# A cross-attention and recurrence kernel: the recurrence's unit changes from four value columns of one chunk to two value columns of two chunks

## The reference, cut to what matters

```
def step(s, rkvw):
    r_t, k_t, v_t, w_t = rkvw
    a = k_t[:, :, :, None] * v_t[:, :, None, :]
    out = jnp.einsum('bhk,bhkd->bhd', r_t, u * a + s)
    return (a + w_t[:, :, :, None] * s, out)
_, outs = jax.lax.scan(step, s0, xs)
```

## Time and profile before

| | before |
|---|---|
| median of 3 runs (lowest, highest) | 2302.81 us (2302.04, 2303.87) |
| the profiled execution | 2301.0 us |
| its span, first to last instruction | 2299.2 us |
| mean granted TensorE clock | 0.967 |
| PE busy | 2141.9 us (93%), 14176 records |
| DVE busy | 1952.8 us (85%) |
| ACT busy | 1260.4 us (55%) |
| POOL busy | 585.2 us (25%) |
| DMA, mean | 30 GB/s |

### The profile page before, as it was taken

The page is one execution under the profiler, slowest core; times in us unless marked ns, Lnnn a source line. Parts: engine busy times, 40 slices in busy tenths (PEclk is TensorE's granted clock), DMA queues, the critical chain, the costliest instruction groups (busy, mean ns, idle before and its releaser), DMA issues. The chain is left out here.

```text
span 2299.2 us, 41734 instructions
## 1 busy us (share of the span) xinstructions
PE 2141.9 (93%) x14176; PEld 1477.2 (64%) x14176; DVE 1952.8 (85%) x4863; ACT 1260.4 (55%) x4405; POOL 585.2 (25%) x700
## 2 busy tenths in 40 slices
PE   3698799999999999999999999999999999999866
PEld 2475576767666676767667676766767676666533
DVE  0258898989899898989989898999989899998982
ACT  1736374573838466383746648373755738374312
POOL 1131314222331422232141322224141222314200
PEclk7799899999999999999999999999999999999977
DMA  7100101001010100001010100101010010100000
GB/s 268 35 7 20 31 11 49 11 11 41 11 50 11 49 11 31 21 11 50 11 49 11 48 3 11 50 11 50 11 49 1 11 50 11 50 2 29 1 19 10
DMA packets 48978, 69.88 MB, mean 30 GB/s; under 512 B 20512, under 2 KB 26656, under 8 KB 48768
## 3 DMA queue, kind: packets, MB, share of 16 engines
q1 hardware_dynamic: 48768, 67.21, 8.9%
HBM read 50.42 MB, written 16.78 MB: 29 GB/s over the span
## 5 line engine op out<-in xcount | busy, mean ns | idle before, releaser
L1226 DVE TENSOR_TENSOR_SCAN st<-ws,st 128x256 f32<-128x256 f32 x1024 | 637.4, 686 | 0.1
L862 ACT ACTIVATE probs_or_mixes<-probs_or_mixes,least 128x128 f32<-128x128 f32 x1024 | 398.9, 403 | 117.4 <-DVE least L1173 116.3
L1215 DVE TENSOR_TENSOR st<-bank_pair,kT 128x1016 f32<-128x1016 f32 x256 | 308.0, 1203 | 88.0 <-PE bank_pair L717 88.0
L1236 DVE TENSOR_TENSOR st<-st,rT 128x1024 f32<-128x1024 f32 x256 | 317.9, 1243 | 0.0
L1173 DVE CUSTOM_DVE_ANT_0 probs_or_mixes<-bank,nmask 128x128 f32<-128x128 f32 x1024 | 231.1, 285 | 100.5 <-PE bank L566 76.0
L1108 POOL TENSOR_SCALAR rstd<-rstd 128x1 f32<-128x1 f32 x96 | 26.5, 276 | 1098.4 <-ACT cin L895 600.1
L1102 POOL TENSOR_TENSOR probs_or_mixes<-probs_or_mixes 128x512 f32<-128x512 f32 x160 | 190.1, 1218 | 341.4 <-DVE probs_or_mixes L1267 341.4
L862 ACT ACTIVATION_READ_ACCUMULATOR probs_or_mixes<-probs_or_mixes,least 128x1 f32 x1024 | 206.4, 202 | 0.0
L717 PE MATMUL bank_pair<-v_hi,sel 32*128 32x256 f32 x1024 | 193.8, 339 | 10.9 <-DVE st L1215 10.6
L717 PE MATMUL bank_pair<-v_lo,sel 32*128 32x256 f32 x1024 | 166.6, 286 | 0.0
L717 PEld LDWEIGHTS bank_pair<-v_hi,sel 32*128 32x128 f32 x1024 | 114.5, 185 | 72.3 <-issue 35.4
(11 more groups left out here) (150 smaller groups left out, 4216.3 us busy)
## 6 DMA issues: line engine op xcount, KB each, us to landing
inputs_turned<-in_ctx_turned SPq DMA_DIRECT2D x16, 512.0 KB, 3.6
inputs_turned<-in_x_turned SPq DMA_DIRECT2D x16, 512.0 KB, 4.6
xin<-in_x SPq DMA_DIRECT2D x16, 512.0 KB, 3.7
x<-xin SPq DMA_DIRECT2D x16, 512.0 KB, 4.1
keep<-x SPq DMA_DIRECT2D x16, 512.0 KB, 3.6
out<-keep SPq DMA_DIRECT2D x32, 256.0 KB, 2.0
wo<-in_wo SPq DMA_DIRECT2D x2, 1024.0 KB, 11.3
nmask<-in_mask SPq DMA_DIRECT2D x16, 128.0 KB, 4.1
```

The source lines that it names most:

```text
L862: last = fn(pr[:, n % 4, j, :], pr[:, n % 4, j, :], ACT.Exp, bias=least[:, n, j:j + 1], scale=-1.0, accum_out=rsum[:, n, j:j + 1])
L1215: tt(dst, src, over(kv, DU, 1), ALU.mult).then_inc(outer.sem, 1)
L1226: last = nc.vector.tensor_tensor_scan(v, ws[:, c].rearrange("p b t -> p (b t)"), v, 0.0, ALU.mult, ALU.add)
L1236: tt(v, v, over(rT[:, u // PER, :], DU, 1), ALU.mult).then_inc(weighed.sem, 1)
```

## The change

**The unit.** A unit is now two value columns (`UNIT_D`) of two chunks (a half of the group's four chunks, called p). It still has 4 x 256 columns in a slot and there are still 16 units in a group, but a slot is now two rows of 512 columns, and a matmul or a scan covers both chunks of one value column at once. The spread is four matmuls of 512 columns instead of eight of 256, the scan two of 512 instead of four of 256, and the reduce four matmuls of 512 instead of eight of 256, into the whole of bank 7, over four reduces instead of two. The bonus moves to the ring of banks as a job of its own, twice a group with two matmuls, and the readout is done twice a group, at 512 columns, instead of four times. POOL's `rk` and `dg` are done in two pieces of 512 instead of four of 256, as two separate steps (`rk`, `joined`).

**Waits.** The first reduce of a half waits until the last readout has read bank 7 (`read_out`). The centred value weights at the start use banks 7 and 3 in turn instead of 7 and `pair`, so that the third matmul group waits for the first copy, the fourth for the second, and PE waits for all four copies before it goes on to `low` (before, it waited for them only at the first `proj_v`).

**Order.** All four lists are new. They are turned round (the period is cut at another place, so that some steps lost one of their lateness), and steps have moved against each other.

```diff
-UNIT_D = [(0, 1, 8, 9), (4, 5, 12, 13), (2, 3, 10, 11), (6, 7, 14, 15)]
+HALF_T = 2 * T
+UNIT_D = [(4 * (w % 2) + w // 2, 8 + 4 * (w % 2) + w // 2) for w in range(2 * PER)]
...
-reduce.4+2 spread.12+2 low_rank.0+1 spread.13+2 key.0 reduce.5+2 tdecay.0+1 spread.14+2 low_rank.2+1 proj_r.0+1
+low_rank.0+1 key.0 spread.13+2 tdecay.0+1 reduce.5+2 low_rank.2+1 spread.14+2 proj_r.0+1 decay.0+1 spread.15+2
...
-            if n % 2 == 0:
-                jobs.append((("readout", n // 2), READOUT, late))
+            keys = [("bonus", n // PER)] if n % PER == PER - 1 else []
...
-        spare = [bank[7][:], pair[:, 0], pair[:, 1], bank[7][:]]
+        spare = [bank[7][:], bank[3][:], bank[7][:], bank[3][:]]
...
-                    if e == 3:
-                        pe.wait_ge(centred_v, 1)
+                    if e >= 2:
+                        pe.wait_ge(centred_v, e - 1)
...
+                pe.wait_ge(centred_v, NC)
...
-                for k in range(2):
-                    for part in (v_hi, v_lo):
-                        for s in range(2):
-                            d = UNIT_D[u % PER][2 * s + k]
-                            r = slice(32 * (d // 4), 32 * (d // 4) + 32)
-                            last = mm(pair[:, s, k * T:(k + 1) * T], sel[r, d % 4, :], part[r, c, :],
-                                      start=part is v_hi, stop=part is v_lo)
+                p, w = u // (2 * PER), u % (2 * PER)
+                for part in (v_hi, v_lo):
+                    for half in range(2):
+                        d = UNIT_D[w][half]
+                        r = slice(32 * (d // 4), 32 * (d // 4) + 32)
+                        last = mm(pair[:, half, :], sel[r, d % 4, :],
+                                  part[r, 2 * p:2 * p + 2, :].rearrange("p c n -> p (c n)"),
+                                  start=part is v_hi, stop=part is v_lo)
...
-                m, c = q % 2, q // 2
+                p, m = q // PER, q % PER
                 if m == 0:
-                    bonus(g, c)
+                    wait(pe, read_out.sem, read_out.after(g, p))
+                if m == PER - 1:
+                    bonus(g, p)
                 pe.wait_ge(weighed.sem, weighed.after(g, 2 * q + 2))
...
+                for half in range(2):
                     for u in (2 * q, 2 * q + 1):
...
+                        r = 64 * half + 32 * (u % 2)
+                        last = mm(bank[7][r:r + 32, :], ebase[:, o:o + 32],
+                                  st[:, u % SLOTS, half * HALF_T:(half + 1) * HALF_T], start=m == 0, stop=m == PER - 1)
...
-                for s in range(DU):
-                    v = st[:, u % SLOTS, s * T:(s + 1) * T]
-                    last = nc.vector.tensor_tensor_scan(v, ws[:, c].rearrange("p b t -> p (b t)"), v, 0.0,
+                for half in range(2):
+                    v = st[:, u % SLOTS, half * HALF_T:(half + 1) * HALF_T]
+                    last = nc.vector.tensor_tensor_scan(v, ws[:, 2 * p:2 * p + 2].rearrange("p c b t -> p (c b t)"), v, 0.0,
...
-                tt(dg[:, c % 2, :], ps[:, T:2 * T], dg[:, c % 2, :], ALU.mult).then_inc(diag.sem, 1)
-                dve.wait_ge(diag.sem, diag.after(g, c + 1))
-                tt(att[:, c, :], ps[:, 0:T], dg[:, c % 2, :], ALU.add).then_inc(free, 1)
+                tt(dg[:], ps[:].rearrange("p (c n) -> p c n", c=2), dg[:], ALU.mult).then_inc(free, 1)
+                dve.wait_ge(summed.sem, summed.after(g, PER * (p + 1)))
+                dve.wait_ge(free, XB.through(("bonus", p), g))
+                tt(att[:, both, :], bank[7][:].rearrange("p (c n) -> p c n", c=2), dg[:], ALU.add).then_inc(read_out.sem, 1)
```

More of the change, by code:

```diff
@@ L127 @@
-values.1 turn_p.8 score.12 turn_p.9 turn_p.10 reduce.2+1 turn_p.11 score.14 spread.8+1 project.0 turn_m.1+2 values.2
-turn_p.12 turn_p.13 spread.9+1 turn_p.14 reduce.3+1 flip.1 turn_p.15 spread.10+1 share.1 values.3 project.1 ffn_k.0+2
-ffn_r.0+2 ffn_k.1+2 spread.11+1 ffn_r.1+2 turn_n.0 turn_n.1 ffn_v.0+2 ffn_v.1+2 low.0
+low_rank.0+1 key.0 spread.13+2 tdecay.0+1 reduce.5+2 low_rank.2+1 spread.14+2 proj_r.0+1 decay.0+1 spread.15+2
+proj_v.0+1 proj_k.0+1 reduce.6+2 decay.1+1 spread.0+1 reduce.7+2 query.0 var.0+2 proj_r.1+1 value.0 score.0
@@ new lines @@
+spread.1+1 rstd.0+2 proj_g.0+1 spread.2+1 score.2 proj_g.1+1 spread.3+1 query.1 turn_p.0 turn_p.1 reduce.0+1 score.4
+spread.4+1 turn_p.2 out.0+2 turn_p.3 spread.5+1 score.6 turn_p.4 out.1+2 values.0 reduce.1+1 score.8 spread.6+1
+turn_p.5 turn_p.6 proj_v.1+1 proj_k.1+1 turn_p.7 turn_m.0+2 spread.7+1 score.10 flip.0 reduce.2+1 values.1 turn_p.8
+score.12 turn_p.9 spread.8+1 share.0 turn_p.10 score.14 turn_p.11 spread.9+1 turn_m.1+2 project.0 reduce.3+1 values.2
+turn_p.12 turn_p.13 turn_p.14 flip.1 turn_p.15 share.1 values.3 spread.10+1 project.1 ffn_k.0+2 ffn_k.1+2 spread.11+1
@@ L130 @@
+ffn_r.0+2 ffn_r.1+2 turn_n.0 turn_n.1 ffn_v.0+2 ffn_v.1+2 low.0 reduce.4+1 spread.12+1
 """
 ACT_ORDER = """
[L133 to L141, removed]
+first.12+2 first.13+2 key.0 state.0+1 tdecay.0+1 first.14+2 first.15+2 proj_r.0+1 proj_v.0+1 square.0+2 state.1+1
@@ new lines @@
+decay.0+1 first.0+1 proj_k.0+1 decay.1+1 square.1+2 proj_r.1+1 query.0 first.1+1 proj_g.0+1 first.2+1 state.2+1
+score.0 score.1 proj_g.1+1 row2.0+2 score.2 first.3+1 query.1 turn_p.0 turn_p.1 score.3 row0.0 turn_p.2 score.4
+first.4+1 turn_p.3 score.5 norm2.0+2 score.6 first.5+1 state.3+1 turn_p.4 score.7 norm2.1+2 first.6+1 turn_p.5
+first.7+1 score.8 apply2.0+2 proj_v.1+1 turn_p.6 apply2.1+2 score.9 proj_k.1+1 turn_p.7 turn_m.0+2 score.10 turn_p.8
+flip.0 score.11 turn_p.9 share.0 turn_p.10 score.12 turn_p.11 score.13 score.14 turn_m.1+2 score.15 turn_p.12
@@ L142 @@
+turn_p.13 turn_p.14 flip.1 turn_p.15 share.1 norm0.0 keep_row.0 first.8+1 first.9+1 apply0.0 row1.0 norm0.1 apply0.1
+ffn_k.0+2 norm1.0 norm1.1 ffn_k.1+2 first.10+1 apply1.0 first.11+1 apply1.1 ffn_r.0+2 ffn_r.1+2 turn_n.0 turn_n.1
+low.0
 """
 POOL_ORDER = """
[L145 to L146 removed]
+negate.0 mix.4+1 rk.0+1 joined.0+1 bias.0 norm2.0+2 bias.1 norm2.1+2 joined.1+1 norm0.0 affine0.0 norm0.1 affine0.1
@@ L147 @@
+norm1.0 norm1.1 mix.0 mix.1 rk.1+1 mix.2 mix.3
 """
 DVE_ORDER = """
[L150 to L153, removed]
@@ L154 @@
-weigh.3+1 score.7 outer.5+1 out.1+2 scan.5+1 score.8 readout.0+1 score.9 inverse.0 outer.6+1 weigh.4+1 proj_v.1+1
-scan.6+1 score.10 score.11 weigh.5+1 outer.7+1 score.12 score.13 gather.0 weigh.6+1 score.14 outer.8+1 score.15
-scan.7+1 inverse.1 project.0 weigh.7+1 outer.9+1 shift2.0+2 gather.1 scan.8+1 project.1 outer.10+1 readout.1+1
-weigh.8+1 scan.9+1 outer.11+1 weigh.9+1 scan.10+1 scan.11+1 shift.0 weigh.10+1 ffn_v.0+2 weigh.11+1 ffn_v.1+2
+outer.0+1 readout.1+2 scan.0+1 var.0+2 value.0 score.0 outer.1+1 score.1 groupnorm.0+2 scan.1+1 outer.2+1 weigh.0+1
@@ L1000, in square @@
             def square(g, p):
-                hold(act, emptied, g, through("readout", 2 * p + 1))
+                act.wait_ge(read_out.sem, read_out.after(g, p + 1))
                 hold(act, filled, g, through("ffn_r", NB - 1, back=1))
```

114 lines of the change are left out of this document (56 added, 58 removed).

## The result

The changed kernel takes 2307.93 us, median of 14 runs (2306.47 to 2314.76), beside 2303.3 us of the kernel before, measured in turn with it (14 runs, 2300.96 to 2304.23). The ratio is 1.0026 with a 95% interval of 1.0018 to 1.0034: slower by 0.26%, where 2290 us and "faster" had been predicted. The profiled execution has a span of 2312.5 us.

The account below looks back on a forecast made before the run. PE was taken to bound the kernel: 14 x (0.4 + 0.35) = 10.5, plus 0.6 and 2.5, less 1.0, gave 12.6 us off 2301.0, so 2288.4 profiled and 2290 us median; range 2265 to 2314 (8 in 10).

Parts of the forecast that it names:

- What bounds the kernel: Middle periods: PE, busy 98.6%, sets the 132.58 us, not DVE; DVE's saving counts only in the drain and PE's waits.
- two of its pieces are merged, nobody waits for them sooner than before. 0: POOL's work, 36 us of a 132.57 us period: merging two pieces was to cost or save nothing.
- DVE to 119.3: DVE's busy time a period was to fall from 121.6 to 119.3 us, by cheaper scans (1.6) and fewer readout instructions (0.7).
- Spread, 0.4 us a period: PE's spread matmuls, 512 columns wide: fewer hand-overs save 0.025 us a unit, 0.4 us a period (0 to 2).
- The rival of an overhead for each matmul: PE's matmuls: each merged hand-over saves 25 ns instead of 2 to 8; 14 us more gain, 2276 us; chance 0.03.
- Form changes, 0.35 us: PE's bonus steps: two fewer changes between tiled and untiled array, 56 to 54, about 0.35 us a period less.
- PE's idle time, left at 1.8: PE's waits in a middle period were to stay at 1.8 us in all, despite the new lists.
- The part for the output projection: Second output projection on PE: the spread ahead of it gives `gather` 0.65 us more against a 0.88 us wait.
- Fill and drain: Start and end: fill loses 1.0 us once, second period gains 0.6, drain gains 2.5 through DVE's scans and readouts.
- no gain: Middle periods: new lists leave PE 0.8 to 1.0 us more idle, spread over many places; 2302 us; chance 0.14.
- The late `flip.0`: ACT comes too late with `flip.0`, PE waits at `share.0`, 2.0 us a period; slower, 2318 us; chance 0.21.
- No idle time at all: Middle periods: with less DVE work PE's 1.8 us of idle time goes, 25 us more gain; 2265 us; chance 0.19.

Follow-up runs that it names:

- experiment 5: Changed kernel with each unit's two scans of 512 columns made as four of 256: 2334.33 us; with `rk.1` also moved behind `mix.3`: 2325.95 us.
- experiment 4: Changed kernel with the spread alone put back to eight matmuls of 256 columns: 2309.61 us, against the changed kernel's 2307.93.
- experiment 1: Changed kernel with all four lists taken back to the order of before, new unit kept: 2326.07 us, ratio 1.0106 to the kernel before.

## Why the prediction was wrong

- **What bounds the kernel:** right that PE does. Wrong was the price of nothing for DVE's work in a middle period ("hidden behind PE and worth nothing by itself"). The prediction named the way out, PE's waits, and then left them at 1.8 us. At 92% busy DVE decides PE's waits at single places, and in the changed lists 3.2 us of its work moved the period by 2.3 (experiment 5).
- **POOL, "two of its pieces are merged, nobody waits for them sooner than before. 0":** the step that failed and turned the sign, since who meets whom was never asked. A product of 512 columns, put by the new list between `mix.1` and `mix.2`, holds a scan up for nearly its whole length (1.02 us). In period terms: 0.82 us (133.10 against 132.28), 11.5 us in 14 periods, 12.8 measured.
- **DVE to 119.3:** its terms are right, 1.125 us a scan and four readout instructions gone, but the scans meet POOL more often. Their lengthening went from 1.0 to 4.1 us a period; the 16 weighs have a mean of 1277 ns, 1242 before, another 0.6 us; one operation of `shift2` and the int32 shift ahead of the Newton steps, lengthened beside POOL too, add 1.1. That makes 119.3 + 3.1 + 0.6 + 1.1 = 124.1 of the 124.39 measured.
- **Spread, 0.4 us a period:** 0 (0.66 us a unit in both; experiment 4). The bounds held it. The rival of an overhead for each matmul falls with it: at 25 ns for each of 32 pairs experiment 4 would have added 0.8 us a period to PE's busy time, and it added 0.03.
- **Form changes, 0.35 us:** the count was off. 56 and 54 are all changes of tiling; between tiled and untiled steps the lists have 46 before and 42 after, and two changes at 0.11 and 0.09 would be 0.2 us, four 0.4. None of it is seen in the sum: PE's busy time is 130.95, not 130.0, and with POOL thinned 130.77, the value of before. At the bonuses part of it is: from start to the next step's start the four took 0.63 + 0.53 + 0.53 + 0.53 us, the two take 1.10 + 0.96, which is 0.15 less. Which other places of the new order took it up is open.
- **PE's idle time, left at 1.8:** 2.15 in the changed kernel, 1.34 with `rk.1` moved. The part for the output projection was right (0.88 to 0.22 us).
- **Fill and drain:** the second period gave 3.9 us where 0.6 was taken, and the lists did it, not the unit (128.16 us in the old order, experiment 1). The drain cost 1.2 where 2.5 were to be gained: its 40 scans take 49.1 us against 50.2 for 80 before, 1276 ns each in place of 1200. The rest of the miss in the drain is open.
- **The rivals:** "no gain" (2302) is nearest in size, not in cause: its idle time was to be spread, here it is one wait. The late `flip.0` is refuted: PE waits for `flipped` 0.2 us in a middle period, at a `turn_p`, 0.31 at most (once, at `share.1`), and never over 0.15 at `share.0`. The outcome of that rival, slower, came about, but by another cause. No idle time at all did not come about.

With `rk.1` moved the kernel stands at 2295.12 us, 5 above the forecast: without that one meeting the direction was right. That it comes so close is in part luck. The terms that were added up for PE's work are not in it; its middle periods gain 0.29 us each by less idle time, which the forecast had left unchanged, and its second period 4.7 us in place of 0.6. In the middle periods what is left is PE's 0.94 us of busy time less 0.46 of idle time, 0.48 x 14 = 6.7 us, and the second period gives some of that back.

## What to carry to other kernels

Before an order is judged, list for each engine which instructions take both operands from SBUF, and lay POOL's steps beside DVE's: what counts is not POOL's load (28% here) but which scan a step meets, how long the step is, and who waits behind that scan. A step merged to save its fixed cost also merges the time for which it holds the other engine up. Nine DVE instructions a period are lengthened by 0.2 us or more; one meeting was 12.8 of the 20 us that thinning three kinds of POOL step gave back, and moving three more steps blindly lost 33 us (2328.66 against 2295.12). Find the one on the chain, and move only that.
